# Which store group sends 256 of its columns by rows from the sync queue, the last or the last but one

## The chip, the cores and the metric

The kernel runs on one core of one Trainium2 chip. The metric is the device time of one execution in microseconds (us), lower is better. Profiles are of one execution each.

## The reference

The input x has 64 batches of 128 channels by 2048 time steps in float32. Each batch has a state number from 0 to 15, and each state has a 128 x 128 weight matrix. The output is x plus the matrix product of the batch with its state's matrix:

```python
def _L0_cond_ref(x, condition, weights):
    W = weights[condition]                      # (64, 128, 128)
    return jnp.einsum('bct,bcd->bdt', x, W)
x = x + _L0_cond_ref(x, itok_B_0_15, L0_cond_weights)   # x: (64, 128, 2048)
```

So 67.1 MB are read and 67.1 MB are written, beside 1 MB of weights.

## The kernel before

On chip, x lives in `x_ring`, a buffer of 20 slots of 2048 columns, with the channels on the 128 partitions; batch b has slot b % 20. Batches are loaded in 13 groups of five (LOAD; the last one, batches 60 to 63, has four) and stored in 16 groups of four (STORE). In memory a load group and a store group are each laid out by channel, so that one row of a transfer is one channel's columns of all batches of the group: 40 KB in a load, 32 KB in a store.

The work of one batch: GpSimd copies the batch's weight matrix out of the table (L109), TensorE multiplies in four pieces of 512 columns into PSUM (L125), VectorE adds the product to x in its slot (L146) and increments `sum_done` of the slot.

What sets the order of the transfers is written out by hand on two queues:

- The sync engine (SP; queue q1 in the profile) issues the weight table and the 13 loads. A load of a group that reuses slots waits (L79) until the stores that held these slots have landed (`room_stored`, one semaphore for each of five rooms; a room is the four slots of a store group, and group s has room s % 5). After the last load SP waits for the sum of the very last batch (L89) and issues two narrow transfers (L91): the last 256 columns of the last store group, first those of channels 0 to 123 and then those of channels 124 to 127. A row of them is 1 KB.
- The scalar engine (ACT; queue q10 in the profile) issues store group s as soon as the sum of its last batch is done (L164). The last group (s = 15, batches 60 to 63, slots 0 to 3, room 0) goes without the 256 columns that SP sends. Group 14 is batches 56 to 59, slots 16 to 19, room 4.

At the end ACT waits, inside the block of the five engines' programs, until all stores of rooms 1 to 4 have landed (L168). Then the five engines meet where the block ends (L71: each drains, and GpSimd collects and releases them). Only behind that meeting ACT waits for room 0, that of the last group (L173), and that is the program's last instruction.

Of the kernel before, what the change touches and what calls it, by code (L numbers as in the profile page):

```python
# [8 lines left out]
RING = 20  # L9
# [5 lines left out]
def groups_of(batches, size):  # L15

    return [(b, min(b + size, batches)) for b in range(0, batches, size)]


def conditioned_residual(nc, x, condition, weights, out, batches, time):  # L20
# [9 lines left out]
    loads, stores = groups_of(batches, LOAD), groups_of(batches, STORE)  # L30
    load_rooms, store_rooms = RING // LOAD, RING // STORE
# [9 lines left out]
    with ExitStack() as ctx:  # L41
        def sbuf(name, shape, dtype=fp32):
            return ctx.enter_context(nc.sbuf_tensor(name, shape, dtype))

        def sem(name):
            return ctx.enter_context(nc.semaphore(name))

        x_ring = sbuf("x_ring", [channels, RING * time])
        weight_table = sbuf("weight_table", [channels, states * features])
        chosen_weights = [sbuf(f"chosen_weights{b}", [channels, features]) for b in range(WEIGHT_SLOTS)]  # L50
        condition_row = sbuf("condition_row", [1, batches], condition.dtype)
        state_row = sbuf("state_row", [1, batches], condition.dtype)
        product = ctx.enter_context(nc.psum_tensor("product", [features, psum_slots, time], fp32))

        condition_loaded = sem("condition_loaded")
        table_loaded = sem("table_loaded")
        states_ready = sem("states_ready")
        x_loaded = [sem(f"x_loaded{r}") for r in range(load_rooms)]
        room_stored = [sem(f"room_stored{r}") for r in range(store_rooms)]

        weights_chosen = [sem(f"weights_chosen{b}") for b in range(per_turn)]
        product_done = [sem(f"product_done{b}") for b in range(per_turn)]
        sum_done = [sem(f"sum_done{b}") for b in range(per_turn)]

        def sums_wanted(turn, b):
            return turn + (2 if b >= per_turn - psum_slots else 1)

        with nc.Block() as block:  # L71
            @block.sync
            def _(sp):
                sp.dma_start(weight_table[:, :], weights.rearrange("c s d -> c (s d)")  # L74
                              ).then_inc(table_loaded, 16)
                for g, (first, end) in enumerate(loads):
                    if first >= RING:
                        for s in stored_for(first, end):
                            sp.wait_ge(room_stored[s % store_rooms], 16 * (s // store_rooms + 1))  # L79
                    b = first % RING  # L80
                    sp.dma_start(x_ring[:, b * time:(b + end - first) * time], rows(x, first, end)
                                 ).then_inc(x_loaded[g % load_rooms], 16)

                first, end = stores[-1]
                turn, b = divmod(end - 1, RING)
                narrow, many = time // 8, channels - 4
                target = rows(out, first, end)
                width = target.shape[1]
                sp.wait_ge(sum_done[b], sums_wanted(turn, b))  # L89
                for part in (slice(0, many), slice(many, channels)):  # L90
                    sp.dma_start(target[part, width - narrow:width],  # L91
                                 x_ring[part, (b + 1) * time - narrow:(b + 1) * time]
                                 ).then_inc(room_stored[(len(stores) - 1) % store_rooms], 16)

            @block.gpsimd
            def _(pool):
                for b in range(per_turn - psum_slots, per_turn):
                    pool.sem_inc(sum_done[b], 1)
                pool.wait_ge(states_ready, 1)
                pool.wait_ge(table_loaded, 16)  # L100

                def choose(turn, count):
                    _, state = nc.values_load_multi_w_load_instructions(
                        state_row[0:1, bass.ds(turn * per_turn, count)],
                        engines=[mybir.EngineType.Pool], min_val=0, max_val=states - 1,
                        skip_runtime_bounds_check_because="state_row is clamped to 0 .. states - 1 on VectorE")
                    for b in range(count):
                        pool.wait_ge(sum_done[(b - psum_slots) % per_turn], turn + 1)
                        pool.tensor_copy(chosen_weights[b % WEIGHT_SLOTS][:, :],  # L109
                                         weight_table[:, bass.ds(state[b] * features, features)]  # L110
                                         ).then_inc(weights_chosen[b], 1)

                with pool.Fori(0, turns) as turn:
                    choose(turn, per_turn)
                choose(turns, rest)

            @block.tensor
            def _(pe):
                def multiply(turn, count):
                    for b in range(count):  # L120
                        if b % LOAD == 0:
                            pe.wait_ge(x_loaded[b // LOAD], 16 * (turn + 1))
                        pe.wait_ge(weights_chosen[b], turn + 1)
                        for m in range(matmuls):
                            last = pe.matmul(  # L125
                                product[:, b % psum_slots, m * BANK_COLUMNS:(m + 1) * BANK_COLUMNS],
                                chosen_weights[b % WEIGHT_SLOTS][:, :],
                                x_ring[:, bass.ds(b * time + m * BANK_COLUMNS, BANK_COLUMNS)],
                                start=True, stop=True)
                        last.then_inc(product_done[b], 1)  # L130

                with pe.Fori(0, turns) as turn:
                    multiply(turn, per_turn)
                multiply(turns, rest)

            @block.vector
            def _(dve):
                dve.wait_ge(condition_loaded, 16)
                dve.tensor_scalar(state_row[0:1, :], condition_row[0:1, :], 0, states - 1,  # L139
                                  AluOpType.max, AluOpType.min).then_inc(states_ready, 1)  # L140

                def add(turn, count):
                    for b in range(count):
                        tile = x_ring[:, bass.ds(b * time, time)]
                        dve.wait_ge(product_done[b], turn + 1)
                        dve.tensor_tensor(tile, product[:, b % psum_slots, :], tile,  # L146
                                          AluOpType.add).then_inc(sum_done[b], 1)

                with dve.Fori(0, turns) as turn:
                    add(turn, per_turn)  # L150
                add(turns, rest)

            @block.scalar
            def _(act):
                act.dma_start(condition_row[0:1, :], condition.rearrange("(o b) -> o b", o=1)
                              ).then_inc(condition_loaded, 16)
                for s, (first, end) in enumerate(stores):
                    turn, last = divmod(end - 1, RING)
                    act.wait_ge(sum_done[last], sums_wanted(turn, last))
                    target = rows(out, first, end)  # L160

                    width = target.shape[1] - (time // 8 if end == batches else 0)
                    column = first % RING * time
                    act.dma_start(target[:, 0:width], x_ring[:, column:column + width]  # L164
                                  ).then_inc(room_stored[s % store_rooms], 16)
                for r in range(store_rooms):
                    if r != (len(stores) - 1) % store_rooms:
                        act.wait_ge(room_stored[r], 16 * len(range(r, len(stores), store_rooms)))  # L168


        def end_of_stores(act):
            room = (len(stores) - 1) % store_rooms
            act.wait_ge(room_stored[room], 16 * (len(range(room, len(stores), store_rooms)) + 2))  # L173

        end_of_stores(nc.scalar)


# [28 lines left out]
```

## Time and profile before

| | |
|---|---|
| median of 3 runs | 319.56 us (319.2 to 319.9) |
| the profiled execution's own time | 319.53 us |
| its span, first to last instruction | 318.1 us |
| TensorE busy (matmul) | 232.0 us, 73% |
| VectorE busy | 146.9 us, 46% |
| GpSimd busy | 19.1 us, 6% |
| DMA, mean over the span | 425 GB/s, 135.29 MB |

Times in the trace run from the span's start. Of the execution's 319.53 us, 1.4 us lie outside the span. In the DMA views a "packet" is one row of a transfer as one of the 16 DMA engines moves it, or the 4-byte increment of a semaphore by which an engine reports the end of its part; a packet is counted in the stretch in which it starts. A share of 100% means 16 busy engines; since a packet's whole time is booked where it starts, short stretches can show more.

### The profile page before, as it was taken

To read this page: it belongs to the slowest core of one execution; us is meant where nothing else is said; L and a number is where in the kernel's file an instruction comes from. 1 tells how busy PE (TensorE), PEld (TensorE's weight loads), DVE (VectorE), ACT (ScalarE), POOL (GpSimd) and SP (SyncE) were. 2 spreads that over 40 slices of the span, in tenths; PEclk is the share of its full clock that TensorE was granted. 3 is DMA by queue.
4 is the path that set the end of the run, shared out by engine and by line. 5 is a ranking of instruction groups with operands and counts; after the bars stand their busy time and mean duration, and the time that the engine had idled before them with its cause. 6 is when DMAs were issued, how large, how long until landed. Compare 5 with 4: busy or idle time off the path is not lost.

```text
span 318.1 us, 1343 instructions
## 1 busy us (share of the span) xinstructions
PE 232.0 (73%) x512; PEld 100.1 (31%) x512; DVE 146.9 (46%) x65; POOL 19.1 (6%) x69
## 2 busy tenths in 40 slices
PE   0079999999902997977979910996995987979400
PEld 0034444444401443423434400442432433434100
DVE  0017667667620374770674730265562564555500
POOL 0000100100000000000000000000000000100000
PEclk9999999999985899995999985899997999999955
DMA  7999999999999999999999999999999999999997
GB/s 307 484 412 412 412 367 441 448 407 461 433 433 404 445 445 445 428 408 457 420 428 453 448 392 446 419 461 424 454 431 397 437 441 449 408 457 400 462 421 313
DMA packets 4460, 135.29 MB, mean 425 GB/s; under 512 B 490, under 2 KB 618, under 8 KB 618
## 3 DMA queue, kind: packets, MB, share of 16 engines
q1 hardware_dynamic: 2152, 68.29, 50.2%
q10 hardware_dynamic: 2306, 66.98, 48.8%
q8 instruction: 1, 0.02, 0.0%
q14 instruction: 1, 0.01, 0.0%
HBM read 68.16 MB, written 67.11 MB: 425 GB/s over the span
## 4 chain that ended last, share of the span: by engine, by line
DMA 65%; PE 26%; DVE 3%; issue 0%; SPq 0%
DMA out<-x_ring 33%; DMA x_ring<-x 32%; PE product L125 26%; DVE x_ring L146 3%; SPq L74 0%; SPq L79 0%
## 5 line engine op out<-in xcount | busy, mean ns | idle before, releaser
L125 PE MATMUL product<-x_ring,chosen_weights 128*128 128x512 f32 x512 | 232.0, 615 | 65.8 <-DMA x_ring<-x 65.8
L146 DVE TENSOR_TENSOR x_ring<-product,x_ring 128x2048 f32<-128x2048 f32 x64 | 146.7, 2292 | 151.3 <-PE product L125 151.3
L125 PEld LDWEIGHTS product<-x_ring,chosen_weights 128*128 128x128 f32 x512 | 100.1, 197 | 196.8 <-issue 113.7
L109 POOL COPY chosen_weights<-weight_table 128x128 f32 x64 | 18.9, 296 | 274.3 <-DVE x_ring L146 267.1
L139 DVE TENSOR_SCALAR state_row<-condition_row 1x64 int32<-1x64 int32 x1 | 0.2, 182 | 2.0 <-DMA condition_row<-condition 2.0
L183 POOL MEMSET const-float32-0.0<- 128x1 f32 x1 | 0.1, 100 | 0.1
L183 POOL MEMSET const-bfloat16-1.0<- 128x1 bf16 x1 | 0.1, 103 | 0.0
L183 POOL MEMSET const-uint8-127<- 128x1 uint8 x1 | 0.1, 102 | 0.0
L183 POOL MEMSET const-float32-1.0<- 128x1 f32 x1 | 0.1, 100 | 0.0
L183 POOL BASE_LOAD x1 | 0.0, 17 | 0.1
## 6 DMA issues: line engine op xcount, KB each, us to landing
x_ring<-x SPq DMA_DIRECT2D x12, 5120.0 KB, 30.0
out<-x_ring ACTq DMA_DIRECT2D x15, 4096.0 KB, 35.9
x_ring<-x SPq DMA_DIRECT2D x1, 4096.0 KB, 28.3
out<-x_ring ACTq DMA_DIRECT2D x1, 3968.0 KB
weight_table<-weights SPq DMA_DIRECT2D x1, 1024.0 KB, 4.9
out<-x_ring SPq DMA_DIRECT2D x1, 124.0 KB
condition_row<-condition ACTq DMA_DIRECT2D x1, 0.2 KB
out<-x_ring SPq DMA_DIRECT2D x1, 4.0 KB
```

What stands on the lines that cost most here:

```text
L109: pool.tensor_copy(chosen_weights[b % WEIGHT_SLOTS][:, :], weight_table[:, bass.ds(state[b] * features, features)]).then_inc(weights_chose ...
L125: last = pe.matmul(product[:, b % psum_slots, m * BANK_COLUMNS:(m + 1) * BANK_COLUMNS], chosen_weights[b % WEIGHT_SLOTS][:, :], x_ring[:, ...
L139: dve.tensor_scalar(state_row[0:1, :], condition_row[0:1, :], 0, states - 1, AluOpType.max, AluOpType.min).then_inc(states_ready, 1)
L146: dve.tensor_tensor(tile, product[:, b % psum_slots, :], tile, AluOpType.add).then_inc(sum_done[b], 1)
L183: nc = bacc.Bacc("TRN2", target_bir_lowering=False, num_devices=1)
```

## The change

The 256 columns that SP sends by rows of 1 KB are taken from the last but one store group (14) in place of the last (15), and are its first columns, those of batch 56, in place of the last ones. SP therefore waits for the sum of batch 56 (slot 16) and not for that of batch 63 (slot 3). ACT sends group 14 without these columns and group 15 whole. The two narrow transfers now count for room 4 and no longer for room 0, and so does their part in the waits: the one inside the block on room 4 wants 16 x (3 + 2), the one behind the block on room 0 only 16 x 4.

```diff
-                first, end = stores[-1]
-                turn, b = divmod(end - 1, RING)
+                first, end = stores[-2]
+                turn, b = divmod(first, RING)
                 narrow, many = time // 8, channels - 4
                 target = rows(out, first, end)
-                width = target.shape[1]
                 sp.wait_ge(sum_done[b], sums_wanted(turn, b))
                 for part in (slice(0, many), slice(many, channels)):
-                    sp.dma_start(target[part, width - narrow:width],
-                                 x_ring[part, (b + 1) * time - narrow:(b + 1) * time]
-                                 ).then_inc(room_stored[(len(stores) - 1) % store_rooms], 16)
+                    sp.dma_start(target[part, 0:narrow], x_ring[part, b * time:b * time + narrow]
+                                 ).then_inc(room_stored[(len(stores) - 2) % store_rooms], 16)
...
-                    width = target.shape[1] - (time // 8 if end == batches else 0)
-                    column = first % RING * time
-                    act.dma_start(target[:, 0:width], x_ring[:, column:column + width]
+                    start = time // 8 if s == len(stores) - 2 else 0
+                    column, width = first % RING * time, target.shape[1]
+                    act.dma_start(target[:, start:width], x_ring[:, column + start:column + width]
                                   ).then_inc(room_stored[s % store_rooms], 16)
                 for r in range(store_rooms):
                     if r != (len(stores) - 1) % store_rooms:
-                        act.wait_ge(room_stored[r], 16 * len(range(r, len(stores), store_rooms)))
+                        narrow_stores = 2 if r == (len(stores) - 2) % store_rooms else 0
+                        act.wait_ge(room_stored[r], 16 * (len(range(r, len(stores), store_rooms)) + narrow_stores))
...
         def end_of_stores(act):
             room = (len(stores) - 1) % store_rooms
-            act.wait_ge(room_stored[room], 16 * (len(range(room, len(stores), store_rooms)) + 2))
+            act.wait_ge(room_stored[room], 16 * len(range(room, len(stores), store_rooms)))
```

On SP, at the end of its program, the order of instructions is the same and the wait in front of the two narrow transfers is another (`sum_done16` is the semaphore of slot 16, `sum_done3` that of slot 3; 124x256 is rows by columns):

```order
 L81 DMA x_ring<-x 128x10240 [waits room_stored4,room_stored3]
 L81 DMA x_ring<-x 128x8192 [waits room_stored0]
-L91 DMA out<-x_ring 124x256 [waits sum_done3]
-L91 DMA out<-x_ring 4x256
+L90 DMA out<-x_ring 124x256 [waits sum_done16]
+L90 DMA out<-x_ring 4x256
 L71 UNCONDITIONAL_BRANCH
```

The narrow transfers now stand behind the last load by one short wait, seven batches earlier than before.

On ACT, the end of its program before the change (the last five stores, and the jump to the block's end with the waits of L168):

```order
L164 DMA out<-x_ring 128x8192 [waits sum_done7]
L164 DMA out<-x_ring 128x8192 [waits sum_done11]
L164 DMA out<-x_ring 128x8192 [waits sum_done15]
L164 DMA out<-x_ring 128x8192 [waits sum_done19]
L164 DMA out<-x_ring 128x7936 [waits sum_done3]
L71 UNCONDITIONAL_BRANCH [waits room_stored3,room_stored4,room_stored2,room_stored1]
```

and of the change:

```order
L162 DMA out<-x_ring 128x8192 [waits sum_done7]
L162 DMA out<-x_ring 128x8192 [waits sum_done11]
L162 DMA out<-x_ring 128x8192 [waits sum_done15]
L162 DMA out<-x_ring 128x7936 [waits sum_done19]
L162 DMA out<-x_ring 128x8192 [waits sum_done3]
L71 UNCONDITIONAL_BRANCH [waits room_stored3,room_stored4,room_stored2,room_stored1]
```

The store that lacks 256 columns moved forward by one; the waits in front of the block's end name the same semaphores, but the one on `room_stored4` now also covers the narrow transfers.

## Rows read from the trace of the kernel before

**Rows 1.** The page's head: the span, DMA over it in 40 slices, the queues

```profile
span 318.1 us, 1343 instructions
...
DMA  7999999999999999999999999999999999999997
...
q1 hardware_dynamic: 2152, 68.29, 50.2%
q10 hardware_dynamic: 2306, 66.98, 48.8%
```

**Rows 2.** The chain that ended last, late pieces: start us, us, what

```profile
255.43 28.34 DMA x_ring<-x
...
283.81 14.02 PE product L125 x32
```

**Rows 3.** Timeline of VectorE: the sums of batches 56, 59 and 63

```profile
271.49 2.29 DVE L146 TENSOR_TENSOR x_ring<-product,x_ring 128x2048 f32<-128x2048 f32 x1 [1.14 <-PE product L125]
...
281.79 2.29 DVE L146 TENSOR_TENSOR x_ring<-product,x_ring 128x2048 f32<-128x2048 f32 x1 [1.14 <-PE product L125]
...
297.84 2.29 DVE L146 TENSOR_TENSOR x_ring<-product,x_ring 128x2048 f32<-128x2048 f32 x1 [1.14 <-PE product L125]
```

**Rows 4.** Timelines of the two queues' issues: store groups 14 and 15, narrow transfers

```profile
284.11 0.34 ACTq L164 DMA_DIRECT2D out<-x_ring  x1
...
300.17 0.34 ACTq L164 DMA_DIRECT2D out<-x_ring  x1
...
300.16 0.78 SPq L91 DMA_DIRECT2D out<-x_ring  x2
```

**Rows 5.** The page's DMA issues: KB each, us from issue to landing

```profile
x_ring<-x SPq DMA_DIRECT2D x1, 4096.0 KB, 28.3
...
out<-x_ring SPq DMA_DIRECT2D x1, 124.0 KB
```

**Rows 6.** DMA queues, 282.1 to 282.7 us: packets, MB, share of 16 engines

```profile
q10 hardware_dynamic: 15, 0.49, 189.5%
q1 hardware_dynamic: 15, 0.00, 1.4%
```

**Rows 7.** DMA queues, 282.7 to 318.2 us

```profile
q10 hardware_dynamic: 498, 14.09, 92.0%
q1 hardware_dynamic: 137, 0.13, 1.1%
```

**Rows 8.** DMA queues, 309 to 315 us

```profile
q10 hardware_dynamic: 83, 2.63, 101.6%
q1 hardware_dynamic: 20, 0.02, 1.0%
```

**Rows 9.** DMA queues, 316.5 to 317.0 us

```profile
q1 hardware_dynamic: 42, 0.04, 24.1%
q10 hardware_dynamic: 1, 0.00, 0.1%
```

**Rows 10.** DMA queues, 317.35 to 317.45 us

```profile
q10 hardware_dynamic: 1, 0.00, 0.6%
```

**Rows 11.** DMA queues, 317.5 to 318.2 us

```profile
q1 hardware_dynamic: 4, 0.00, 1.0%
```

**Rows 12.** Lines L168, L71 and L173: duration ns min/median/max, first and last start us

```profile
L168 ACTq EVENT_SEMAPHORE  x2: 17/28/38, 300.5 to 308.4; - x2
...
L71 ACTq COMPARE_BRANCH  x1: 33/33/33, 308.5 to 308.5; - x1
...
L71 SPq EVENT_SEMAPHORE  x1: 17/17/17, 308.8 to 308.8; - x1
L71 ACTq EVENT_SEMAPHORE  x1: 17/17/17, 308.8 to 308.8; - x1
...
L173 ACTq EVENT_SEMAPHORE  x1: 17/17/17, 318.1 to 318.1; - x1
```

## The prediction

> **What bounds the kernel now.** I read the page's head first. The DMA engines are at 9 of 10 tenths in every slice but the first and the last [rows 1], and the two big queues together take 50.2% + 48.8% = 99.0% of the time of 16 engines. So bytes over DMA set the time, and an instruction matters only where it leaves a DMA engine without work, or where it stands behind the last byte. The change moves no byte to another queue and adds none: 128 rows of 1 KB are sent by SP in both kernels. What can change is the order at the end, so the rest is read there.
>
> The chain that ended last shows how the end begins: the last load is issued at 255.43 us and lands 28.34 us later [rows 2]; it is the one of 4096 KB, so its rows are 32 KB as the stores' are, and the first narrow transfer is the one of 124 KB [rows 5]. When it has landed, TensorE works through the last four batches from 283.81 us [rows 2]. VectorE's rows give the sums [rows 3]: batch 56 is done at 271.49 + 2.29 = 273.78 us, batch 59 at 284.08, batch 63 at 300.13. ACT issues group 14 at 284.11 and group 15 at 300.17, and SP its two narrow transfers at 300.16 [rows 4], so the issues follow the sums at once.
>
> Then I cut the last 36 us into stretches of the DMA view. Three facts come out.
>
> First, how many engines carry the narrow rows. Between 316.5 and 317.0 us almost nothing but narrow packets starts, 42 of them, and they take 24.1% of 16 engines, which is 3.9 [rows 9]. So only four engines carry them (I call them the four), 128 / 4 = 32 rows each, and the other twelve carry none. One narrow row costs 24.1% x 16 x 0.5 us / 42 = 46 ns; 32 cost 1.47 us of one engine.
>
> Second, how an engine chooses between its two queues. From 309 to 315 us 83 wide rows start on 16 engines, 5.2 each, and 20 narrow ones on the four, 5 each [rows 8]. So an engine that has both takes one packet of each in turn, a wide row (101.6% x 16 x 6 us / 83 = 1.18 us) and then a narrow one. The wide ones pay for it: nothing is overlapped, and an engine's end is the sum of its packets.
>
> Third, who is last. The last packet of the wide store, the end report of an engine outside the four, starts at 317.4 us [rows 10]. The last four narrow packets start behind 317.5 us and hold one engine for 1.0% x 16 x 0.7 = 0.11 us [rows 11], so that engine ends at 317.6 us. The program ends at 318.1 [rows 12], 0.5 us after it. The four thus end last, with a lead over the slowest of the others of only 317.6 - 317.4 = 0.2 us.
>
> **The change, part by part.**
>
> *Narrow rows earlier.* SP may issue them at 273.8 us in place of 300.2. But they are queued behind the last load on q1, whose parts end on most engines between 282.1 and 282.7 (the 15 reports of q1 [rows 6]). From there on all that any engine has to do is the rest of groups 12 to 15 and the narrow rows, and store traffic keeps it busy to the end: 498 packets of q10 take 92.0% of 16 engines over 35.5 us [rows 7], the rest being the drained last 2 us. An engine of the four has the same 32 narrow rows behind 282.7 in both kernels, and the same wide bytes: group 14 loses 8 rows of 1 KB there and group 15 gets them back. So its end stays at 317.6 us. No waiting engine is made to wait less: no load follows. This part: 0. Bounds: if a narrow row between two wide ones were free, the four would end up to 32 x 46 ns earlier, but the laggard of the twelve holds the end at 317.4, so the gain is at most 0.2 us; rows 8 and 9 speak against even that, since the wide rate per engine with narrow rows between (5 rounds in 6 us) leaves the turn at 1.2 us. A loss: the wait for a sum could hold up SP, but behind it SP has only the block's end, which it reached behind 300.16 + 0.78 us before too [rows 4]; 0.
>
> *Last group whole.* The twelve get 8 KB more in group 15 and 8 KB less in group 14, both behind 282.7 us: 0.
>
> *The wait on room 4.* Here I see the only term. Before, it ended at 308.4 us (L168), and all five engines were past the block's end by 308.8 (L71) [rows 12], covered by 9 us of stores. Now it also wants the narrow transfers. When do they land? Count turns on one of the four from 282.2 us, where its load part ends. Wide rows left: 15 in the first stretch (one per engine, one engine missing) [rows 6] and 498 less 4 groups x 16 reports = 434 in the second [rows 7]; (15 + 434) / 16 = 28 rows an engine. With four reports that makes 32 turns of q10. The narrow queue has 31 rows, a report, 1 row, a report: 34 turns. By one turn each, the q10 part comes to its last report when the narrow part still has two packets. So the narrow transfers still land last, at 317.6 us, and room 4 is now the last to be complete, about 0.1 us behind room 0. The count could be off by two wide rows and the outcome would be the same; off by three it would not.
>
> Then the block's end stands behind the last byte: from the end of the wait on room 4 (308.4) to the release of all engines (308.8) are 0.4 us. The last wait, on room 0, is then already satisfied. The cover (stores that go on for 9 us) is gone, and the term is +0.4 us in full. The lower end is 0, the case in which a laggard of the twelve ends behind the four; the upper end: what the other four engines do between their release and the end of the execution was also beside the stores before. No row shows it; of the 1.4 us outside the span some part may grow. I bound it by nothing and by another 0.4 us (the same meeting once more), and take 0.05 since ACT had to finish behind 318.1 before as well.
>
> *Sum:* 319.53 (own time of the profiled execution) + 0 + 0 + 0.4 + 0.05 = 319.98, or 320.0 us. The median of the runs is 319.56, so the reference is the same to 0.01%; the change is +0.14%. That is less than the 0.2% (0.64 us) that a measurement of this kernel can tell from no change.
>
> **The rivals.**
>
> *A. The block's end stays hidden (319.5 us, range 319.2 to 319.8).* It needs room 4 complete at least 0.4 us before room 0. Either a laggard among the twelve ends later than 317.6 + 0.4 = 318.0; it is at 317.4 here, and how far it lags may vary between executions (their times do by 0.7 us). Or the narrow rows run ahead of the wide ones: an engine would have to take several of them in one turn. For 309 to 315 us the count is 5 against 5.2, one to one [rows 8], which speaks against it; if it took nine in a turn, 32 rows would need four turns or 5 us and be gone by 288 us. The Trainium skill (DMA: Bandwidth & Descriptors, Queues, rings and completion order) says that an engine drains a whole packet of about 9 to 17 descriptors from one ring before it changes to the next; by that the narrow rows would be through early and the time would be 319.5 us. The trace does not agree for rows of these sizes: one row of each in turn. Chance 0.18, most of it the laggard.
>
> *B. The other side: slower than 320.2 us.* The mechanism is the same meeting at the block's end, at a higher price: all engines but ACT now leave the block at about 318.5 us in place of 308.8, and whatever they do after it is exposed. For it: nothing shows how long that takes, and ACT alone needs no time to speak of. It decides from 0.64 us on, that is 0.4 plus 0.24 of this. Price up to 0.4 + 0.4 + scatter of the runs: 320.2 to 320.7, about 320.4 us. Chance 0.25.
>
> *C. Faster than 318.9 us.* The narrow rows leave the tail, as the last 1.1 us of the trace suggest at first sight (from 316.5 us on hardly more than the four work [rows 9]). It needs the four to end at about 316.5 us, and the laggard too; but every engine's sum of packets is kept. Even with the four out of the way the laggard leaves 0.2 us, 319.3 us. Time if the tail were gone: 319.53 - 1.1 + 0.4 = 318.8 us. Chance 0.05.
>
> **How the numbers follow.** Forecast (319.8 to 320.2 us, block's end exposed): 0.52; A 0.18; B 0.25; C 0.05. The predicted time is the forecast's, 320.0. Range: 319.2 (lower end of A: 319.53 less the 0.2 us of the four's lead and 0.1 of scatter) to 320.7 (upper end of B); outside are C and the far part of B, less than 0.15 together. Faster by over 0.2%: C, 0.05. Slower by over 0.2%: B, 0.25. Within 0.2%: the forecast and A, 0.70.
>
> **What would show it.** In the profile of the changed kernel: ACT issues group 15 at about 300.2 us; narrow packets start at about 282.3 and go on, one for each wide row on four engines, to the very end, so that a stretch 309 to 315 again shows about 20 on q1; the stretch behind 316.5 us holds 31 and 32 KB rows that end, hardly any narrow ones (before: 42 in half a microsecond); the last report still at 317.6. The L71 rows move from 308.8 to about 318.5 us, the wait behind the block follows within 0.1 us, and the span is 318.5 to 318.6. I am wrong if L71 stays well ahead of the last wait (A), if the last DMA packet starts before 317 us (C), or if the span is 318.5 but the time grows by more than 0.2 us beyond it (B).

## The result: 0.3% slower, and the profile after

The changed kernel takes 320.10 us (median of 17 runs, 319.93 to 321.44), the kernel before 319.24 us beside it (17 runs, 318.97 to 320.19). The ratio is 1.0031 with a 95% interval of 1.0021 to 1.0040, so the change costs 0.7 to 1.3 us. (Each ratio in this document is an estimate from all the timed runs, with its interval, and not the quotient of the two medians, which would be 1.0027 here.) The profiled execution took 320.37 us with a span of 318.7.

The page's head shows the same picture as [rows 1]: DMA full from the second slice to the last but one, and the two queues with the same packets and bytes.

```profile
span 318.7 us, 1343 instructions
...
DMA  7999999999999999999999999999999999999996
...
q1 hardware_dynamic: 2152, 68.29, 50.1%
q10 hardware_dynamic: 2306, 66.98, 48.7%
```

The timelines of VectorE (sums of batches 56, 59 and 63) and of the two queues' issues (the narrow transfers, groups 14 and 15), against [rows 3, 4]:

```profile
271.62 2.29 DVE L144 TENSOR_TENSOR x_ring<-product,x_ring 128x2048 f32<-128x2048 f32 x1 [1.14 <-PE product L123]
...
281.92 2.29 DVE L144 TENSOR_TENSOR x_ring<-product,x_ring 128x2048 f32<-128x2048 f32 x1 [1.14 <-PE product L123]
...
299.55 2.29 DVE L144 TENSOR_TENSOR x_ring<-product,x_ring 128x2048 f32<-128x2048 f32 x1 [1.14 <-PE product L123]
...
273.94 0.86 SPq L90 DMA_DIRECT2D out<-x_ring  x2
...
284.25 0.34 ACTq L162 DMA_DIRECT2D out<-x_ring  x1
...
301.87 0.34 ACTq L162 DMA_DIRECT2D out<-x_ring  x1
```

The narrow transfers are issued at 273.94, right behind the sum of batch 56, 26 us earlier than before. Group 15 is issued 1.7 us later than before (301.87 against 300.17), because TensorE's granted clock fell for a few microseconds in this execution: it was 0.50, the lower of its two levels (1.2 GHz), in the stretch 285 to 287 us, where it was 1.00 (2.4 GHz) in the profile before (3 matmuls against 6 in that stretch). In both the engine had sat idle for about 2 us (1.93 and 2.05) until the last load landed, and matrix work began at 283.8 us. The later issue of group 15 costs nothing, since group 14 was still in the queue when group 15 came (over the stretch 309 to 315 us below, q10 holds 99.8% of 16 engines).

The DMA queues in the stretch 309 to 315 us, then 316.5 to 317.0, then 317.45 to 317.5, then 317.5 to 318.7 us (packets, MB, share of 16 engines), against [rows 8 to 11]:

```profile
q10 hardware_dynamic: 79, 2.59, 99.8%
q1 hardware_dynamic: 20, 0.02, 1.0%
...
q1 hardware_dynamic: 8, 0.00, 2.8%
q10 hardware_dynamic: 2, 0.00, 0.2%
...
q1 hardware_dynamic: 2, 0.00, 6.9%
q10 hardware_dynamic: 2, 0.00, 2.2%
...
q1 hardware_dynamic: 1, 0.00, 0.0%
```

Narrow rows still go until the end, one for each wide row on four engines: 20 of them in six microseconds, as before. Only the tail of narrow rows is gone, 8 packets between 316.5 and 317.0 us in place of 42. But the last packet has hardly moved: it starts just behind 317.5 us, before at 317.6, and it is one of q1's. The DMA work ends where it did, within 0.1 us.

What has moved is the meeting of the engines. The lines of the wait inside the block (L167), of the block's end (L71) and of the wait behind it (L172), against [rows 12]:

```profile
L167 ACTq EVENT_SEMAPHORE  x2: 17/28/38, 302.3 to 318.2; - x2
...
L71 ACTq COMPARE_BRANCH  x1: 33/33/33, 318.3 to 318.3; - x1
...
L71 SPq EVENT_SEMAPHORE  x1: 17/17/17, 318.6 to 318.6; - x1
L71 ACTq EVENT_SEMAPHORE  x1: 17/17/17, 318.6 to 318.6; - x1
...
L172 ACTq EVENT_SEMAPHORE  x1: 17/17/17, 318.7 to 318.7; - x1
```

Before, the engines were released at 308.8 us and ACT's last wait ended at 318.1 alone. Now the wait on room 4 ends at 318.2, the meeting follows until 318.6, and the last wait, already satisfied, at 318.7. The time outside the span grew as well: 1.69 us (median over the 17 runs of each run's time less its span, 1.64 to 1.74). It was 1.4 us in the profiled execution before, and 1.40 us is the median over 35 runs of the kernel before beside the first experiments (1.35 to 1.46). The two ranges do not overlap, so the late leave shows in each of the 17 runs. The 17 runs of the kernel before that were timed beside the change have no spans on record.

### The profile page after: what moved, and what is told of

The parts are those of the page before. It is cut to its first block, busy times and chain, and to the rows that moved or that the text cites. A ratio compares the mean times of both kernels' runs of the same rounds, so it can differ in the third digit from the quotient of the medians.

```text
span 318.7 us, 1343 instructions
## 1 busy us (share of the span) xinstructions
PE 236.3 (74%) x512; PEld 101.8 (32%) x512; DVE 146.8 (46%) x65; POOL 18.9 (6%) x69
## 4 chain that ended last, share of the span: by engine, by line
DMA 64%; PE 27%; DVE 3%; issue 0%; SPq 0%
DMA out<-x_ring 32%; DMA x_ring<-x 32%; PE product L123 27%; DVE x_ring L144 3%; SPq L74 0%; SPq L79 0%
## 5 line engine op out<-in xcount | busy, mean ns | idle before, releaser
L123 PE MATMUL product<-x_ring,chosen_weights 128*128 128x512 f32 x512 | 236.3, 624 | 63.2 <-DMA x_ring<-x 63.2
L123 PEld LDWEIGHTS product<-x_ring,chosen_weights 128*128 128x128 f32 x512 | 101.8, 201 | 196.9 <-issue 116.4
```

The costliest lines, as they stand in the source:

```text
L123: last = pe.matmul(product[:, b % psum_slots, m * BANK_COLUMNS:(m + 1) * BANK_COLUMNS], chosen_weights[b % WEIGHT_SLOTS][:, :], x_ring[:, ...
```

## The experiments

Each was timed in turns with the kernel before, on the same chip as it. "Outside" is a run's time less its span, the median over the experiment's runs. For spans I also give means, since a run's span is on record to 0.1 us only. Three groups of experiments shared three sets of runs of the kernel before: medians 319.59 (35 runs), 319.57 (22) and 319.47 us (33), outside 1.40, 1.41 and 1.41 us.

### 1. The change with its wait behind the block

```diff
-                    if r != (len(stores) - 1) % store_rooms:
-                        narrow_stores = 2 if r == (len(stores) - 2) % store_rooms else 0
-                        act.wait_ge(room_stored[r], 16 * (len(range(r, len(stores), store_rooms)) + narrow_stores))
+                    if r not in ((len(stores) - 1) % store_rooms, (len(stores) - 2) % store_rooms):
+                        act.wait_ge(room_stored[r], 16 * len(range(r, len(stores), store_rooms)))
...
         def end_of_stores(act):
+            room = (len(stores) - 2) % store_rooms
+            act.wait_ge(room_stored[room], 16 * (len(range(room, len(stores), store_rooms)) + 2))
             room = (len(stores) - 1) % store_rooms
```

> The changed kernel with its transfers as they are, but the wait on room 4 moved behind the block, ahead of that on room 0. Theory 1 (the block's end is exposed, the order of the transfers is free): all of the loss comes back, 319.2 to 319.4 us, a ratio to the kernel before of 0.9995 to 1.0005; the last L71 event back at about 308.8 us, the time outside the span back from 1.7 to 1.4 us. Theory 2 (narrow rows among the wide ones cost something themselves): 0.2 us or more stay, ratio 1.0007 or above, with the last DMA packet later than in the kernel before (317.6 us).

Measured: 319.54 us (12 runs), ratio 0.9994 (0.9981 to 1.0006), outside 1.41 us. The time is back to that of the kernel before, so theory 2 is not needed; its 1.0007 lies just outside the interval, and the last DMA packet of the profile starts at 317.6 us, as in the kernel before. The last L71 event and the wait behind the block:

```profile
L71 ACTq EVENT_SEMAPHORE  x1: 17/17/17, 300.2 to 300.2; - x1
...
L173 ACTq EVENT_SEMAPHORE  x1: 234/234/234, 318.1 to 318.1; - x1
```

The expected 308.8 us for L71 was a slip: with room 4 out of the block nothing in it waits for group 14, and the engines meet once group 15 is issued.

### 2. The kernel before with its wait inside the block

```diff
                 for r in range(store_rooms):
                     if r != (len(stores) - 1) % store_rooms:
                         act.wait_ge(room_stored[r], 16 * len(range(r, len(stores), store_rooms)))
+                room = (len(stores) - 1) % store_rooms
+                act.wait_ge(room_stored[room], 16 * (len(range(room, len(stores), store_rooms)) + 2))
```

> The kernel before with its transfers as they are, but the wait on room 0 moved into the block, so that the engines meet behind the last store. Theory 1: the whole loss appears without any move of a transfer, 320.0 to 320.2 us, a ratio of 1.0025 to 1.0030, of it about 0.5 us in the span and 0.3 outside. Theory 2: only a part of the loss, ratio 1.0020 or less, since the transfers' order, which is not changed here, carries the rest.

Measured: 320.41 us (12 runs), ratio 1.0020 (1.0008 to 1.0032), outside 1.69 us. No transfer was moved, and the loss is there, 0.3 to 1.0 us. The interval alone does not tell theory 1's 1.0025 from theory 2's limit; the two parts do: the mean span is 318.61 us against 318.23 of the kernel before (+0.38) and the time outside 1.69 against 1.40 (+0.29), close to the changed kernel's, timed in another set of runs (mean span 318.65, outside 1.69). The rows of the wait (L170) and of the meeting:

```profile
L170 ACTq EVENT_SEMAPHORE  x1: 38/38/38, 318.3 to 318.3; - x1
...
L71 ACTq EVENT_SEMAPHORE  x1: 17/17/17, 318.7 to 318.7; - x1
...
L175 ACTq EVENT_SEMAPHORE  x1: 17/17/17, 318.8 to 318.8; - x1
```

### 3. All five engines wait behind the block

```diff
         end_of_stores(nc.scalar)
+        end_of_stores(nc.sync)
+        end_of_stores(nc.gpsimd)
+        end_of_stores(nc.tensor)
+        end_of_stores(nc.vector)
```

> The kernel before, and behind the block not ACT alone but all five engines wait for the last store. The meeting at the block's end stays hidden. It takes apart the two parts of the price: if the time outside the span grows because the other engines leave late, then the span stays at 318.1 us and the time outside it goes from 1.4 to 1.7 us, in all +0.3 us, ratio 1.0009. If the time outside grows for another reason (the meeting itself), no change: ratio 0.9998 to 1.0003.

Measured: 319.91 us (12 runs), ratio 1.0012 (1.0001 to 1.0024), outside 1.76 us (1.70 to 1.81). The meeting is hidden here and the mean span is unchanged at 318.23 us, yet 0.36 us are lost outside the span. So the part outside comes from engines that leave late, not from the meeting. In the profiled execution the meeting is at 308.8, and engines leave at 318.9:

```profile
L71 ACTq EVENT_SEMAPHORE  x1: 17/17/17, 308.8 to 308.8; - x1
...
L173 SPq EVENT_SEMAPHORE  x1: 17/17/17, 318.9 to 318.9; - x1
L173 ACTq EVENT_SEMAPHORE  x1: 17/17/17, 318.9 to 318.9; - x1
```

The 318.9 is this execution's (one of the four engines had its last narrow packets between 318.3 and 318.6 us); over the 12 runs the median span is 318.15.

### 4. The narrow rows left out

```diff
-                sp.wait_ge(sum_done[b], sums_wanted(turn, b))
-                for part in (slice(0, many), slice(many, channels)):
-                    sp.dma_start(target[part, 0:narrow], x_ring[part, b * time:b * time + narrow]
-                                 ).then_inc(room_stored[(len(stores) - 2) % store_rooms], 16)
...
-                        narrow_stores = 2 if r == (len(stores) - 2) % store_rooms else 0
+                        narrow_stores = 0
```

> The changed kernel without its two narrow transfers: the first 256 columns of batch 56 are not stored at all, 0.13 MB of 67 MB less. Room 4 then lands with the wide store of group 14, at about 308 us, and the block's end is hidden. Theory 1: the end is then set by a lagging one of the twelve other engines, 317.4 to 317.5 us for the last packet, so 319.1 to 319.2 us, ratio 0.9993 to 0.9998. If the four engines' 32 narrow rows each (1.5 us) were the bound, and no engine lagged, it would be 1.2 us less, ratio 0.996.

Measured: 319.13 us (12 runs), ratio 0.9985 (0.9974 to 0.9996), outside 1.41 us. The median span is 317.7 us, against 318.2. The gain of about 0.5 us (0.1 to 0.8) is small beside the 1.5 us that the rows cost each of four engines, so others do hold the end, as expected; but it may be more than the 0.2 us that the one trace allowed. Its last packet is a report of q10; the stretch 317.45 to 317.6 us:

```profile
q10 hardware_dynamic: 1, 0.00, 0.4%
```

### 5. Seventeen turns in place of thirty-four

```diff
-                for part in (slice(0, many), slice(many, channels)):
+                for part in (slice(0, 68),):
...
-                        narrow_stores = 2 if r == (len(stores) - 2) % store_rooms else 0
+                        narrow_stores = 1 if r == (len(stores) - 2) % store_rooms else 0
```

> The changed kernel, wait on room 4 inside the block as it is, but with only one narrow transfer, of channels 0 to 67; the 256 columns of the other 60 channels of batch 56 are not stored at all. 68 rows go to four engines, 17 each. It tests the count of turns: one narrow row for each wide one from 282.3 us on means that the last narrow one goes at 282.3 + 17 x 1.26 = 304 us, so room 4 lands with its wide store at about 308 us, the last L71 event comes at about 308.8 us although the wait stands in the block, and the time outside the span is 1.4 us; 319.1 to 319.5 us in all. If an engine with two queues gave the narrow one fewer turns than one in two, or if the place of the wait alone set the price, L71 would stay at 318 us or later and the time outside at 1.7.

Measured in a single run: 319.12 us, span 317.7, outside 1.42 us. The queues from 283 to 300 us, from 300 to 304 us with that view's count of packets in front, then from 304 to 310 us, where q1 has no row any more, and the meeting:

```profile
q10 hardware_dynamic: 255, 7.26, 99.0%
q1 hardware_dynamic: 63, 0.06, 1.1%
...
DMA packets 59, 1.59 MB, mean 398 GB/s; under 512 B 4, under 2 KB 9, under 8 KB 9
...
q1 hardware_dynamic: 9, 0.01, 0.4%
...
q10 hardware_dynamic: 96, 2.59, 100.1%
...
L71 ACTq EVENT_SEMAPHORE  x1: 17/17/17, 308.4 to 308.4; - x1
...
L172 ACTq EVENT_SEMAPHORE  x1: 17/17/17, 317.7 to 317.7; - x1
```

That q1's rows are on four engines shows in its 63 + 9 = 72 packets: 68 rows and four end reports (the four packets under 512 B), one for each engine. From 283 to 300 us q10 has 255 packets on 16 engines, 16 each, and q1 63 on four, also 16 each: one for one again. Seventeen rows an engine are through by 304 us, room 4 is complete with its wide store, and the meeting is hidden although its wait stands in the block. The 15 rows an engine that were left out are only 0.7 us of its work (46 ns each), and the meeting came 10 us earlier. So it is the number of turns that exposes the meeting in the changed kernel, together with the place of the wait.

### 6. SP waits as well as ACT

```diff
         end_of_stores(nc.scalar)
+        end_of_stores(nc.sync)
```

> The kernel before, and behind the block ACT and SP wait for the last store; the other three engines leave at about 308.8 us. The kernel before has 1.40 us outside the span, the one in which all five wait has 1.76. Theory 1 (what is exposed is how many engines or which one leaves late): with SP alone added it is between the two, 1.4 to 1.6 us. Theory 2 (any second engine that leaves late brings the whole price): 1.7 us or more.

Measured in a single run: 319.5 us, span 318.1, outside 1.40 us. SP's late leave adds nothing to ACT's that shows beside the scatter of 0.06 us, and theory 2 falls; so does theory 1 where it goes by the number of late engines alone.

### 7. One engine waits, each in turn

```diff
-        end_of_stores(nc.scalar)
+        end_of_stores(nc.tensor)
```

and the same with `nc.vector`, `nc.gpsimd` and `nc.sync`.

> The kernel before, but the wait for the last store behind the block is TensorE's and not ACT's, so TensorE alone leaves at 318.1 us and the other four at about 308.8. With ACT and SP late the time outside the span was 1.40 us, as with ACT alone; with all five late 1.76, and 1.69 in the changed kernel. So the extra 0.29 to 0.36 us comes from TensorE, VectorE or GpSimd. If a single late engine brings it, one of these three runs has 1.7 us and the others 1.4; if it takes several of them together, each has about 1.4 to 1.5.

> The same with VectorE as the only engine that waits behind the block. Same reading: 1.7 us outside the span if VectorE's late leave is what costs, 1.4 if not.

> The same with GpSimd as the only engine that waits behind the block. Same reading: 1.7 us outside the span if GpSimd's late leave is what costs, 1.4 if not.

> The same with SP as the only engine that waits behind the block; ACT leaves at 308.8 us. If each engine that leaves last has its own price, SP's may be under ACT's 1.40 us outside the span, which would make this the fastest version: 319.2 to 319.5 us, ratio 0.998 to 0.9995. If SP and ACT are alike, ratio 0.9995 to 1.0005 and 1.40 us outside.

| the engine that leaves last | outside, us | us | ratio (95%) |
|---|---|---|---|
| SP | 1.25 (1.20 to 1.30) | 319.17 | 0.9992 (0.9982 to 1.0002) |
| VectorE | 1.37 (1.34 to 1.42) | 319.50 | 0.9994 (0.9984 to 1.0005) |
| ACT (the kernel before) | 1.41 (1.34 to 1.47) | 319.47 | 1 |
| TensorE | 1.54 (1.47 to 1.59) | 319.51 | 0.9997 (0.9987 to 1.0007) |
| GpSimd | 1.78 (1.73 to 1.83) | 319.93 | 1.0012 (1.0001 to 1.0022) |

GpSimd alone brings the price of all five (1.76), and SP is 0.16 us cheaper than ACT. No run changes only GpSimd's leave in the changed kernel; that its 1.69 us there has this cause is inferred from the table. The ranges of the time outside do not overlap between SP, ACT and GpSimd, so these steps are clear there, while only GpSimd's shows in the ratio. The version with SP as the waiter has the lowest median of all that store everything, but its interval includes 1, so it isn't shown to beat the kernel before.

### 8. No narrow rows, everything stored

```diff
-                sp.wait_ge(sum_done[b], sums_wanted(turn, b))
-                for part in (slice(0, many), slice(many, channels)):
-                    sp.dma_start(target[part, width - narrow:width],
-                                 x_ring[part, (b + 1) * time - narrow:(b + 1) * time]
-                                 ).then_inc(room_stored[(len(stores) - 1) % store_rooms], 16)
...
-                    width = target.shape[1] - (time // 8 if end == batches else 0)
+                    width = target.shape[1]
```

The wait behind the block wants 2 x 16 less.

> The kernel before without narrow transfers, group 15 stored whole by ACT, everything stored. Leaving the narrow columns out of the changed kernel gave 0.9985 of the kernel before, 0.45 us less. Storing them by 16 engines costs each 8 KB more, 8 x 1 KB / 32 KB x 1.21 us = 0.3 us. Theory 1 (the four engines end last in most executions, by more than the 0.2 us of the profiled one): 319.4 us, ratio 0.9990 to 1.0000. Theory 2 (lagging engines among the twelve set the end, so their relief by 8 KB is worth its 0.3 us): 319.7 to 319.9 us, ratio 1.0003 to 1.0010.

Measured: 319.70 us (11 runs), ratio 1.0003 (0.9994 to 1.0013). The two theories' ranges meet where it lies, and it tells only this: sending 256 columns by rows, as the kernel before does, gains no more than 0.4 us, and possibly nothing.

### 9. Relief for two engines

```diff
-                narrow, many = time // 8, channels - 4
+                narrow, many = time // 2, channels - 2
...
-                    width = target.shape[1] - (time // 8 if end == batches else 0)
+                    width = target.shape[1] - (time // 2 if end == batches else 0)
```

> The kernel before with other narrow transfers: 1024 columns, rows of 4 KB, first channels 0 to 125 and then 126 and 127. 126 rows should go to 14 engines, 9 each, and 2 rows to two engines, so two engines lose 32 KB (1.2 us) and the others gain 4 or 8 KB (0.15 to 0.3 us). If the two engines that lag by 1 us at the end are the two relieved ones, the end comes 0.5 to 0.9 us earlier, 318.7 to 319.1 us, ratio 0.997 to 0.9985. If the laggards are others, 0.1 to 0.4 us later, ratio 1.0003 to 1.0013.

Measured: 319.98 us (12 runs), ratio 1.0015 (1.0005 to 1.0025), so 0.2 to 0.8 us later, on the side of other laggards. Two reports of q10 come early, between 314.2 and 315 us (first line, the two packets under 512 B; all eight packets of this stretch are q10's), 1 us ahead of the next; and the last packets, 317.4 to 318.3 us, are two other reports of q10:

```profile
DMA packets 8, 0.17 MB, mean 215 GB/s; under 512 B 2, under 2 KB 2, under 8 KB 2
...
q10 hardware_dynamic: 2, 0.00, 0.1%
```

The two that finish early are the two that were relieved of 1.2 us, and two others still end late. So in this execution the laggards are among the 14 that carry more. Which of them lag, and why, stays open.

## Why the prediction was right or wrong

**The time** was forecast as 320.0 us and is 320.10; the range of 319.2 to 320.7 held it. That the two are so close is luck. The change was forecast as +0.45 us on 319.53 and measured as 0.7 to 1.3 us, about double; but the kernel before took 319.24 us beside it, 0.3 us less than in the profiled execution, and the two errors nearly cancel. The kind of outcome was not the likeliest one either: 0.70 stood on "within 0.2%" and 0.25 on slower by more, and it is 0.31% slower. The forecast's mechanism and that of rival B are one, the meeting at the block's end; B had its price right: 320.2 to 320.7 us is 0.7 to 1.2 above 319.53.

**Narrow rows earlier: 0.** Right. The last packet starts at 317.5 us, before at 317.6, and experiment 1, the same transfers with the wait elsewhere, is within 0.9981 to 1.0006 of the kernel before. **Turns.** Right: one narrow row for each wide row, 20 in the stretch 309 to 315 again, and the narrow queue's last report behind the wide one's. Experiment 5 halves the turns and hides the meeting. But the order at the end is a close one: the stretch 317.45 to 317.5 us above holds two reports of q10, so q10's last one starts less than 0.1 us ahead of q1's.

**The wait on room 4: +0.4 us in the span.** Right. The released engines moved from 308.8 to 318.6 us. In the one trace the wait inside the block ends at 318.2 and the last instruction follows at 318.7; over the runs the mean span grows by 0.38 us in experiment 2. In the changed kernel it is 318.65, which is 0.42 more than the 318.23 of the 35 runs of the kernel before, but those are another set. For the 17 runs of the kernel before beside the change I can only estimate it: their mean time of 319.35 us less 1.40 is 317.95, and the growth would then be 0.7 us. So the 0.4 rests on experiment 2 and on the traces.

**The part outside the span: taken as 0.05 us.** This is the term that was mis-sized. "I bound it by nothing and by another 0.4 us ... and take 0.05 since ACT had to finish behind 318.1 before as well": it measures 0.29 us (1.69 against 1.40, and the same again in experiment 2). The reason given is unsound, since engines don't cost the same when they leave last. ACT does cost 1.41 us, but GpSimd, which the meeting now also holds until 318.5, costs 1.78 when it alone leaves last (experiment 7). With 0.4 + 0.29 the sum would have been 319.53 + 0.69 = 320.2 us, +0.22%, and "slower by over 0.2%" would have been the likeliest kind. No row of the trace of before has this price; the time outside of the other engines had to be measured.

What the two terms leave of the measured 0.7 to 1.3 us is nothing at the interval's lower end and 0.6 us at the upper; experiment 2, with the same two terms, is 0.3 to 1.0 us. I take the two for the whole, since experiment 1 brings all of the loss back by the place of the wait alone, but a rest of some tenths isn't excluded.

**Rival A** (hidden meeting) came about in none of the 17 runs: each has 1.64 us or more outside its span. The Trainium skill's rule (DMA: Bandwidth & Descriptors, Queues, rings and completion order) of about 9 to 17 descriptors a turn does not hold for these rows, where a descriptor is taken for a row: on each of the four engines 5 narrow rows went in the six microseconds in which about 5 wide ones did, in both traces, and 16 beside 16 in experiment 5. **Rival C** had its bound too tight: "at most 0.2 us" was one execution's lead of the four over the next engine. With the rows left out, 0.1 to 0.8 us are gained (experiment 4).

## What to carry to other kernels

When a transfer is moved from one completion semaphore to another, follow the waits on both, and look where they stand in the program: a wait that only closes the program costs nothing while stores cover it, and the price of all that stands behind it once it is the last to be satisfied. Issuing a transfer early does not make it land early; on a DMA engine with two busy queues it advances one row for each row of the other, so count its rows against the other's. And the time outside the span is part of the metric: let GpSimd leave early, and wait for the last store on another engine (0.4 us here).

## What the runs showed of the hardware

- A DMA engine with rows of 1 KB in one queue and of 32 KB in the other took one of each in turn (20 on four engines beside 79 to 83 on sixteen in 6 us; 63 beside 255 in 17 us), so a queue's progress goes by its number of rows and not by its bytes.
- A transfer of 124 rows ran on four engines (24.1% of 16), and so did one of 68 rows, by its four end reports. The Trainium skill (DMA: Bandwidth & Descriptors, Why a DMA increments its semaphore by 16 and not by 1) gives the rule: the largest number up to 16 that divides the slowest dimension of both sides, here the rows. The traces agree for 124 and 68.
- The meeting of the five engines took 0.4 us from the end of ACT's wait to the release (308.4 to 308.8 us before, 318.2 to 318.6 in the changed kernel).
- The time outside the span depended on which engine left last, from 1.25 us (SP) to 1.78 us (GpSimd), steady within 0.07 us of the median over 8 to 33 runs each.
- A granted clock of TensorE of 0.50 for a few microseconds (285 to 287 us, where it had been 1.00 before) went with last sums that were 1.7 us later in the changed kernel's trace. The end of the DMA work did not move.
